# First row group's second edges loaded as float8 by pairs of units, and the packed exponentials' upper half written by ScalarE

## The chip, the cores and the metric

The kernel runs on one core of one Trainium2 chip. The metric is the device time of one execution in microseconds, the median of the runs. TensorE is called PE, VectorE DVE, ScalarE ACT, GpSimd POOL and the queue of SyncE SP. 16 DMA engines move the data of all queues.

## What is computed

A graph attention layer over 8192 nodes with 128 features, its input normalised and rectified first, and its output added to the input:

```python
    h = jnp.maximum(_layernorm(x, axis=-1), 0.0)
    Wh = h @ W
    a1, a2 = (a[:Fout, 0], a[Fout:, 0])
    f1 = Wh @ a1
    f2 = Wh @ a2
    e = jax.nn.leaky_relu(f1[:, None] + f2[None, :], negative_slope=ALPHA)
    e = jnp.where(adj == 0, -jnp.inf, e)
    attention = jax.nn.softmax(e, axis=1)
    h_prime = attention @ Wh
    x = x + h_prime
```

`x` is 8192 x 128 float32 (4.2 MB), `adj` is 8192 x 8192 int32 (268 MB) and holds only 0 and 1. ALPHA is 0.2.

## The kernel before

**Tiling.** The 8192 rows of the output are cut into 16 row groups `q` of 512 rows, four rows (`PACK`) to each of the 128 partitions. The 8192 columns of a group are cut into 16 units `b` of 512 columns. For one unit DVE writes four tiles of weights (L987: the larger of two packed exponentials, and the smaller of that and the mark of the edge), and PE multiplies them into the four accumulators `acc` (L476 and L480, 16 of each in a unit), which takes 16 x 4 x 4 products in a group.

**Edges.** POOL's queue loads `adj` and turns the int32 into one byte on the way. In `masks` the four rows of a partition lie side by side. The edges of two rows are put into one byte and summed as integers on POOL (`mix`, L274, for the first group; `mix4` and `join` for the later ones), PE transposes the sums (L458), and ACT spreads them into `marks` (`unpack`, L685). For this the bytes of the two rows of a pair must carry different values. In the first group all four rows arrive as uint8 (0 or 1), one unit at a time (`load_part`, L256, 128 x 4 x 512 bytes), and ACT multiplies the rows of the second half by 200 (`second`, L702) before POOL adds. In later groups `load_half` loads the second of each pair as float8 already, whose 1.0 is the byte 60.

**The first group does more than the others.** While it runs, PE also makes the features of all nodes (L440 and the transposes L422), DVE takes the statistics of `x` (`statistics`, L913) and finishes the inverses of the deviation (`inverses`, L928 to L937), ACT takes roots, rectifies, copies `wh` out of PSUM and takes exponentials, and POOL normalises (L283) and scales (`scaled`, L330). `x` comes in six loads on SP's queue (L200), of 1, 1, 2, 2, 4 and 6 tiles of 512 rows; the last three wait until the edges of units 0, 1 and 3 have landed. I call them x3, x4 and x5. `statistics(4)` needs x3, `statistics(6)` x4 and `statistics(10)` x5.

**The packed exponentials.** For tile `g` ACT writes eight exponentials per partition into `exps` (L675) and four more into `tmp` (L676), which signals `exps_ready`. DVE's `pack` makes the upper half of `packed` from `exps` with a multiplication (L965), waits for itself, and makes the lower half from both (L966). POOL's `scaled` waits for `exps_ready` too; ACT's `high_part` (L764) waits for `scaled`, and ACT's `root`, for which DVE's `inverses` waits, stands behind `high_part`.

**Order.** Every engine's program is written out by hand. DVE's in unit `b` of the first group is: weights of unit `b+1` (in two halves, with `inverses` between the halves where `b+1` is 2, 5 or 9), `low_part` (L974), `pack(b+2)`, statistics. PE starts the products of unit `b` only when `low_part(b)` is done (`pair_ready`).

## Time and profile before

| | us |
|---|---|
| median of 3 runs | 772.83 (772.83 to 774.30) |
| the profiled execution, device time | 773.42 |
| its span, first to last instruction | 771.5 |

| engine | busy us | share of the span |
|---|---|---|
| PE (matmul) | 751.3 | 97% |
| PE (weight load) | 687.7 | 89% |
| DVE | 726.5 | 94% |
| ACT | 579.2 | 75% |
| POOL | 442.9 | 57% |

The time outside the span is 773.42 - 771.5 = 1.9 us. The clock granted to PE was 0.999 of full speed over the span. Of the chain that ended last 91% is PE's, 4% DVE's, 2% ACT's. The share of a whole span says little here: the first row group (to about 93 us) and the other fifteen have different limits, so that the tables are to be read by stretches.

### The profile page before, as it was taken

To read this page: it belongs to the slowest core of one execution; us is meant where nothing else is said; L and a number is where in the kernel's file an instruction comes from. 1 tells how busy PE (TensorE), PEld (TensorE's weight loads), DVE (VectorE), ACT (ScalarE), POOL (GpSimd) and SP (SyncE) were. 2 spreads that over 40 slices of the span, in tenths; PEclk is the share of its full clock that TensorE was granted. 3 is DMA by queue.
4 is the path that set the end of the run, shared out by engine and by line. 5 is a ranking of instruction groups with operands and counts; after the bars stand their busy time and mean duration, and the time that the engine had idled before them with its cause. 6 is when DMAs were issued, how large, how long until landed. Compare 5 with 4: busy or idle time off the path is not lost.

```text
span 771.5 us, 23891 instructions
## 1 busy us (share of the span) xinstructions
PE 751.3 (97%) x8676; PEld 687.7 (89%) x8676; DVE 726.5 (94%) x1183; ACT 579.2 (75%) x1139; POOL 442.9 (57%) x501
## 2 busy tenths in 40 slices
PE   6899899999999999999999999999999999999997
PEld 5789789999999999999999999999999999999986
DVE  6998899999999999999999999999999999999996
ACT  5889887777778777777877777777777777777762
POOL 8787865646646664664666456465655646564510
PEclk9999999999999999999999999999999999999999
DMA  9999899999999999999999999999999999997100
GB/s 171 179 105 108 85 114 128 108 114 120 107 126 100 116 93 113 108 100 114 97 121 94 118 97 99 112 104 121 90 120 93 99 111 102 115 97 82 19 15 18
DMA packets 48246, 79.70 MB, mean 103 GB/s; under 512 B 2834, under 2 KB 11732, under 8 KB 48212
## 3 DMA queue, kind: packets, MB, share of 16 engines
q0 software_dynamic: 41088, 67.12, 90.5%
q1 hardware_dynamic: 6976, 12.09, 4.6%
q8 instruction: 17, 0.28, 0.1%
q14 instruction: 17, 0.14, 0.1%
q10 hardware_dynamic: 148, 0.07, 0.0%
HBM read 276.37 MB, written 4.23 MB: 364 GB/s over the span
## 4 chain that ended last, share of the span: by engine, by line
PE 91%; DVE 4%; ACT 2%; DMA 1%; POOL 1%; issue 1%; DVEq 0%; ACTq 0%; POOLq 0%
PE acc L476 56%; PE acc L480 29%; PE stage L467 4%; DVE wt_ring L987 2%; PE stage L440 1%; DMA masks<-in_adj_dram 1%; DVE pairs L974 1%; PE stage L422 0%; ACT marks L727 0%; DVE stats L913 0%; PE stage L458 0%; POOL tmp L330 0%; POOL masks L274 0%; DVE xm L1082 0%; ACT wh L649 0%
## 5 line engine op out<-in xcount | busy, mean ns | idle before, releaser
L476 PE MATMUL acc<-pairs,wt_ring 128*128 128x258 f16 x4096 | 717.5, 274 | 4.9 <-DVE pairs L974 3.5
L987 DVE SCALAR_TENSOR_TENSOR wt_ring<-stage,packed,marks 128x512 f32<-128x512 f32 x1024 | 688.4, 744 | 30.9 <-PE acc L480 21.5
L480 PE MATMUL acc<-pairs,wt_ring 128*128 128x129 f16 x4096 | 697.7, 220 | 0.0
L476 PEld LDWEIGHTS acc<-pairs,wt_ring 128*128 128x128 f16 x4096 | 398.8, 98 | 56.2 <-DVE pairs L974 5.1
L480 PEld LDWEIGHTS acc<-pairs,wt_ring 128*128 128x128 f16 x4096 | 400.3, 98 | 4.9
L727 ACT ACTIVATE marks<-codes 128x512 uint16<-128x512 uint8 x480 | 274.6, 620 | 12.5
L717 ACT ACTIVATE codes<-stage 128x512 uint16<-128x512 uint8 x240 | 142.8, 595 | 147.1 <-PE stage L467 146.6
L291 POOL DMA_DIRECT2D masks<-in_adj_dram x120 | 87.7, 731 | 219.8 <-PE stage L467 198.9
L310 POOL TENSOR_TENSOR masks<-masks 128x512 int32<-128x512 int32 x120 | 150.6, 1282 | 1.3
L319 POOL TENSOR_TENSOR masks<-masks 128x256 int32<-128x256 int32 x120 | 87.6, 735 | 55.7 <-ACT masks L710 54.8
L710 ACT ACTIVATE masks<-masks 128x512 uint16<-128x512 uint16 x120 | 74.8, 623 | 1.3 <-POOL masks L310 0.7
L467 PE MATMUL stage<-ident,masks 128*128 128x128 f32 x240 | 67.0, 279 | 0.8 <-ACT codes L717 0.4
L467 PEld LDWEIGHTS stage<-ident,masks 128*128 128x128 f32 x240 | 33.7, 141 | 5.0 <-issue 1.5
L337 POOL TENSOR_SCALAR fin<-fin 128x516 f32<-128x516 f32 x15 | 22.8, 1519 | 2.1 <-ACT fin L752 1.6
L330 POOL TENSOR_TENSOR tmp<-wh,tmp 128x512 f32<-128x512 f32 x16 | 18.0, 1124 | 10.0 <-ACT tmp L676 10.0
L440 PE MATMUL stage<-wx,ht 128*128 128x130 f32 x120 | 20.9, 299 | 1.5 <-ACT ht L643 0.7
L283 POOL TENSOR_SCALAR xn<-xm,small 128x128 f32<-128x128 f32 x42 | 19.4, 471 | 4.3 <-DVE small L937 4.3
L752 ACT ACTIVATE fin<-acc 128x258 f32<-128x258 f32 x60 | 19.4, 381 | 0.0
L347 POOL TENSOR_TENSOR xm<-fin,xm 128x512 f32<-128x512 f32 x15 | 18.0, 1199 | 1.8 <-ACT fin L758 1.5
L758 ACT ACTIVATE fin<-fin,inv 128x128 f32<-128x128 f32 x60 | 19.0, 392 | 0.0
L440 PEld LDWEIGHTS stage<-wx,ht 128*128 128x128 f32 x120 | 16.6, 200 | 2.7 <-ACT ht L643 1.1
L685 ACT ACTIVATE marks<-stage 128x1024 uint16<-128x1024 uint8 x16 | 16.3, 1019 | 1.4 <-PE stage L458 1.4
(78 smaller groups left out, 201.3 us busy)
## 6 DMA issues: line engine op xcount, KB each, us to landing
masks<-in_adj_dram POOLq DMA_DIRECT2D x120, 512.0 KB, 9.7
masks<-in_adj_dram POOLq DMA_DIRECT2D x16, 256.0 KB, 21.9
out_dram<-xm SPq DMA_DIRECT2D x15, 256.0 KB, 7.8
ht<-e_words SPq DMA_DIRECT2D x14, 256.0 KB, 8.5
xm<-in_x_dram SPq DMA_DIRECT2D x1, 1536.0 KB, 13.4
xm<-in_x_dram SPq DMA_DIRECT2D x2, 512.0 KB, 6.6
xm<-in_x_dram SPq DMA_DIRECT2D x1, 1024.0 KB, 9.8
xm<-in_x_dram SPq DMA_DIRECT2D x2, 256.0 KB, 3.1
```

The lines of the kernel that those rows point to most:

```text
L291: nc.gpsimd.dma_start(to[:, c * PACK + h:(c + 1) * PACK:2, :], adj_half[q, c, :, h::2, :]).then_inc(adj_second[c] if h else adj_loaded[c], 16)
L310: nc.gpsimd.tensor_tensor(edges4[:, c, :, 0, sl], edges4[:, c, :, 0, sl], edges4[:, c, :, 1, sl], ALU.add).then_inc(s["mixed4"], 1)
L319: nc.gpsimd.tensor_tensor(edges4[:, c, 0, 0, sl], edges4[:, c, 0, 0, sl], edges4[:, c, 1, 0, sl], ALU.add).then_inc(s["joined"], 1)
L337: nc.gpsimd.tensor_scalar(fin[:, :, E1:2 * E1], fin[:, :, E1:2 * E1], 1.0 / LOW, None, ALU.mult).then_inc(s["lows_scaled"], 1)
L440: mm = nc.tensor.matmul(to[:, r * 256:r * 256 + WC], ht[:, g % 2, k:k + P], wx[:], start=(r == 0), stop=(r == 1), skip_group_check=True)
L467: nc.tensor.transpose(stage[:, 0, 0:P], words[:, c * PACK, kk * P:(kk + 1) * P], ident[:]).then_inc(s["transposed"], 1)
L476: return nc.tensor.matmul(acc[:, r, 0:2 * E1], wtv[:, w, r, 1, :], pairv[:, t, :, 0:E1], start=st, stop=end)
L480: return nc.tensor.matmul(acc[:, r, E1:2 * E1], wtv[:, w, r, 0, :], pairv[:, t, 0, 0:E1], start=False, stop=False)
L710: nc.scalar.activation(twos[:, c, 1, 0, sl], twos[:, c, 1, 0, sl], ACT.Copy, scale=2.0).then_inc(s["doubled"], 1)
L717: nc.scalar.activation(codes2[:, b % 2, :].rearrange("p (s w) -> p s w", s=PACK), stage[:, 0, 0:P].bitcast(U8).rearrange("p (w s) -> p s w ...
L727: mm = nc.scalar.activation(split[:, b % MR, :].rearrange("p (s a w) -> p a s w", s=PACK, a=2)[:, h], codes[:, b % 2, :].rearrange("p (s w ...
L987: nc.vector.scalar_tensor_tensor(out=wtq[:, t % NW], in0=e_row, scalar=packed[:, t, 1:2], in1=edges[:, k], op0=ALU.max, op1=ALU.min).then_ ...
```

## The change

The rows of the second half are loaded as float8 (byte 60 for an edge), so that `second` goes; `SPLIT` becomes 256/60 for `unpack`. A load now covers one unit for units 0 and 1 and two units from there (`UNITS`), and is made of two DMAs, one for each half of the rows, that add to one semaphore (32). The counts before and behind POOL's other work (`EARLY`, `PARTS`) are in loads. ACT writes the upper half of `packed` with an exponential of its own (bias `log(SCALE * CUT)`), between the two that it had; DVE's multiplication goes.

```diff
-CUT = 1.0 - 2.0 ** -11
+CUT = 1.0 - 2.0 ** -11 - 2.0 ** -16
...
-SECOND = 200.0
-SPLIT = 256.0 / SECOND
+ONE8 = 60.0
+SPLIT = 256.0 / ONE8
...
-    EARLY = 10
+    EARLY = 5
...
-    PARTS = {0: (12,), 1: (13,), 2: (14, 15)}
+    PARTS = {0: (6,), 1: (7,), 2: (8,)}
+
+    UNITS = [(0, 1), (1, 2)] + [(u, u + 2) for u in range(2, UN, 2)]
...
-        adj_first = adj.rearrange("(q p s) (b k) -> q b p s k", p=P, s=PACK, k=BANK)
+        adj_first = adj.rearrange("(q p s) k -> q p s k", p=P, s=PACK)
...
-            for k, part in ((3, 0), (4, 1), (5, 3)):
-                sp.wait_ge(first_loaded[part], 16)
+            for k, part in ((3, 0), (4, 1), (5, 2)):
+                sp.wait_ge(first_loaded[part], 32)
                 load_x(k)
...
-            def load_part(u):
-                c, k = u // KC, u % KC
-                nc.gpsimd.dma_start(masks[:, c * PACK:(c + 1) * PACK, k * BANK:(k + 1) * BANK],
-                                    adj_first[0, u]).then_inc(first_loaded[u], 16)
+            def load_part(k):
+                lo, hi = UNITS[k]
+                c = lo // KC
+                at, to = (lo - c * KC) * BANK, (hi - c * KC) * BANK
+                for h, tiles in ((0, masks), (1, masks8)):
+                    sl = slice(HALF * h, HALF * (h + 1))
+                    nc.gpsimd.dma_start(tiles[:, c * PACK + HALF * h:c * PACK + HALF * (h + 1), at:to],
+                                        adj_first[0, :, sl, lo * BANK:hi * BANK]).then_inc(first_loaded[k], 16)
...
-                pool.wait_ge(first_loaded[u], 16)
-                pool.wait_ge(s["second_ready"], u + 1)
+                pool.wait_ge(first_loaded[part_of(u)], 32)
...
                 nc.scalar.activation(exps, wh[:, sl, Fo:WC], ACT.Exp, scale=1.0 - SLOPE, bias=cst[:, 0:1])
+                nc.scalar.activation(packedv[:, sl, :, 1], wh[:, sl, Fo:WC], ACT.Exp, scale=1.0 - SLOPE,
+                                     bias=cst[:, 3:4])
                 nc.scalar.activation(tmp[:, g % 2, :, Fo:E1], wh[:, sl, E1:WC], ACT.Exp, scale=-1.0,
                                      bias=cst[:, 1:2]).then_inc(s["exps_ready"], 1)
...
-            def second(b):
-
-                c, k = b // KC, b % KC
-                act.wait_ge(first_loaded[b], 16)
-                sl = slice(k * BANK // 2, (k + 1) * BANK // 2)
-                nc.scalar.activation(twos[:, c, 1, :, sl], twos[:, c, 1, :, sl], ACT.Copy, scale=SECOND
-                                     ).then_inc(s["second_ready"], 1)
...
-                then(nc.vector.tensor_scalar(packedv[:, sl, :, 1], exps, CUT / LOW, None, ALU.mult))
```

All calls of `second` go from ACT's program. POOL's program from its first load on, in the kernel before (a row is a line, its operation, its tiles, its shape and how many stand in a row):

```order
L256 DMA masks<-in_adj_dram 128x4x512 x2
L261 MEMSET ident 128x128
L263 ISA
L263 AFFINE_SELECT ident<-ident 128x128
L256 DMA masks<-in_adj_dram 128x4x512 x8
L274 TENSOR_TENSOR masks<-masks 128x2x128
L330 TENSOR_TENSOR tmp<-wh,tmp 128x4x128
L283 TENSOR_SCALAR xn<-xm,small 128x128 x6
L274 TENSOR_TENSOR masks<-masks 128x2x128
L330 TENSOR_TENSOR tmp<-wh,tmp 128x4x128
L256 DMA masks<-in_adj_dram 128x4x512 x2
L274 TENSOR_TENSOR masks<-masks 128x2x128
```

and in the changed one, where the loads are on L264, `mix` on L280, `scaled` on L336 and the normalisation on L289:

```order
L264 DMA masks<-in_adj_dram 128x2x512 x2
L268 MEMSET ident 128x128
L270 ISA
L270 AFFINE_SELECT ident<-ident 128x128
L264 DMA masks<-in_adj_dram 128x2x512 x2
L264 DMA masks<-in_adj_dram 128x2x1024 x6
L280 TENSOR_TENSOR masks<-masks 128x2x128
L336 TENSOR_TENSOR tmp<-wh,tmp 128x4x128
L289 TENSOR_SCALAR xn<-xm,small 128x128 x6
L280 TENSOR_TENSOR masks<-masks 128x2x128
L336 TENSOR_TENSOR tmp<-wh,tmp 128x4x128
L264 DMA masks<-in_adj_dram 128x2x1024 x2
```

The number of DMAs ahead of the first `mix` is ten in both, and now they cover eight units in place of ten. Behind the third and the fourth `scaled` one DMA stood in the kernel before; now two stand there.

ACT's program in the loop's first round (`b` = 0), in the kernel before, from `high_part(1)` to the normalisation of tile 4:

```order
L764 ACTIVATE pairs<-tmp 128x4x129
L649 ACTIVATE wh<-stage 128x260
L702 ACTIVATE masks<-masks 128x2x256
L776 ACTIVATE small<-stats,cst 128x8
L779 ACTIVATE small<-small 128x8
L643 ACTIVATE ht<-stage 128x512
L649 ACTIVATE wh<-stage 128x260
L675 ACTIVATE stage<-wh,cst 128x8
L676 ACTIVATE tmp<-wh,cst 128x4
L685 ACTIVATE marks<-stage 128x1024
L702 ACTIVATE masks<-masks 128x2x256
L635 ACTIVATE xn<-xm,small 128x128
```

and in the changed one:

```order
L762 ACTIVATE pairs<-tmp 128x4x129
L654 ACTIVATE wh<-stage 128x260
L774 ACTIVATE small<-stats,cst 128x8
L777 ACTIVATE small<-small 128x8
L648 ACTIVATE ht<-stage 128x512
L654 ACTIVATE wh<-stage 128x260
L680 ACTIVATE stage<-wh,cst 128x8
L681 ACTIVATE packed<-wh,cst 128x8
L683 ACTIVATE tmp<-wh,cst 128x4
L692 ACTIVATE marks<-stage 128x1024
L640 ACTIVATE xn<-xm,small 128x128
```

The two `second` (L702) are gone, and the new exponential (L681) stands ahead of the one that signals `exps_ready`, and ahead of the unpacking of the marks.

## Rows read from the trace of the kernel before

**Rows 1.** Windows: start:end, length; PE, PEld, DVE, ACT, POOL busy; PEclk; DMA; GB/s

```profile
15.00:30.00 15.00, 11.01 (x97) 8.81 (x95) 13.39 (x36) 12.42 (x32) 11.45 (x18) 1.00 1.16 206
30.00:45.00 15.00, 13.49 (x139) 12.33 (x140) 14.76 (x37) 12.59 (x30) 12.28 (x19) 1.00 1.21 137
...
97.00:760.00 663.00, 662.97 (x7822) 608.96 (x7823) 638.21 (x969) 499.81 (x956) 365.13 (x386) 1.00 0.95 101
```

**Rows 2.** Timeline of PE, 15 to 65 us: start, us, instruction, idle before it

```profile
30.47 0.28 PE L476 MATMUL acc<-pairs,wt_ring 128*128 128x258 f16 x1 [1.65 <-DVE pairs L974]
...
44.89 0.29 PE L476 MATMUL acc<-pairs,wt_ring 128*128 128x258 f16 x1 [0.86 <-DVE pairs L974]
...
63.01 0.28 PE L476 MATMUL acc<-pairs,wt_ring 128*128 128x258 f16 x1 [0.57 <-DVE pairs L974]
```

**Rows 3.** Timeline of DVE, 15 to 45 us, same columns

```profile
16.87 1.43 DVE L913 BATCH_NORM_STATS2 stats<-xm 128x6 f32<-128x256 f32 x4
19.03 2.73 DVE L987 SCALAR_TENSOR_TENSOR wt_ring<-stage,packed,marks 128x512 f32<-128x512 f32 x4 [0.73 <-ACT marks L685]
...
23.38 1.42 DVE L913 BATCH_NORM_STATS2 stats<-xm 128x6 f32<-128x256 f32 x4
24.71 1.39 DVE L987 SCALAR_TENSOR_TENSOR wt_ring<-stage,packed,marks 128x512 f32<-128x512 f32 x2
26.02 0.33 DVE L928 TENSOR_SCALAR small<-stats 128x8 f32<-128x8 f32 x1
...
28.10 1.40 DVE L987 SCALAR_TENSOR_TENSOR wt_ring<-stage,packed,marks 128x512 f32<-128x512 f32 x2
29.42 0.99 DVE L974 SCALAR_TENSOR_TENSOR pairs<-pairs,tmp 128x516 f16<-128x516 f16 x1
...
34.51 0.17 DVE L965 TENSOR_SCALAR packed<-stage 128x8 f16<-128x8 f32 x1
34.71 0.17 DVE L966 SCALAR_TENSOR_TENSOR packed<-packed,stage 128x8 f16<-128x8 f16 x1
34.79 1.44 DVE L913 BATCH_NORM_STATS2 stats<-xm 128x6 f32<-128x256 f32 x4
```

**Rows 4.** Timeline of ACT: `second` of unit 2; the exponentials behind 56.5 us

```profile
20.00 0.62 ACT L702 ACTIVATE masks<-masks 128x512 uint16<-128x512 uint16 x1
...
56.99 0.27 ACT L675 ACTIVATE stage<-wh,cst 128x8 f32<-128x8 f32 x1
57.20 0.29 ACT L676 ACTIVATE tmp<-wh,cst 128x4 f32<-128x4 f32 x1
```

**Rows 5.** Timeline of POOL, 20 to 30 us

```profile
20.77 0.72 POOL L274 TENSOR_TENSOR masks<-masks 128x256 int32<-128x256 int32 x1 [0.95 <-ACT masks L702]
...
28.81 1.05 POOL L330 TENSOR_TENSOR tmp<-wh,tmp 128x512 f32<-128x512 f32 x1 [0.39 <-ACT tmp L676]
```

**Rows 6.** Windows of three mixtures of transfers (last two columns: DMA share, GB/s)

```profile
13.50:21.00 7.50, 6.31 (x48) 5.32 (x47) 6.74 (x14) 6.30 (x18) 6.09 (x11) 1.00 1.13 241
...
36.00:40.00 4.00, 3.82 (x42) 3.37 (x41) 3.97 (x10) 3.75 (x9) 3.98 (x7) 1.00 1.24 105
127.00:133.00 6.00, 6.00 (x73) 5.51 (x72) 5.93 (x10) 4.02 (x8) 4.26 (x5) 1.00 1.06 163
```

**Rows 7.** Line L200, x3 with x4, then x5: issue, and time to landing

```profile
L200 SPq DMA_DIRECT2D xm<-in_x_dram x2: 380/383/386, 9.8 to 12.3; - x2
...
DMA to landing us min/median/max: 6.9/8.3/9.8
...
L200 SPq DMA_DIRECT2D xm<-in_x_dram x1: 381/381/381, 21.7 to 21.7; - x1
...
DMA to landing us min/median/max: 13.4/13.4/13.4
```

**Rows 8.** Line L256, the loads of units 2 and 3: duration of the issue, landing

```profile
L256 POOL DMA_DIRECT2D masks<-in_adj_dram x2: 742/758/774, 4.0 to 4.8; - x2
...
DMA to landing us min/median/max: 12.2/14.6/17.0
```

More of the change, by code:

```diff
@@ L50 @@
 SCALE = 0.015
-CUT = 1.0 - 2.0 ** -11
+CUT = 1.0 - 2.0 ** -11 - 2.0 ** -16
 TOP = 512.0
 NORM = 1.01
-SECOND = 200.0
-SPLIT = 256.0 / SECOND
+ONE8 = 60.0
+SPLIT = 256.0 / ONE8
 ABOVE = 0.1
-ONE8 = 60.0
 APART = 64.0
@@ L100, in batch_of, with part_of @@
         return next(k for k, (lo, hi) in enumerate(BATCHES) if lo <= g < hi)
+    def part_of(u):
+        return next(k for k, (lo, hi) in enumerate(UNITS) if lo <= u < hi)
     with ExitStack() as ctx:
@@ L128, in gat_kernel @@
         a_row = sb("a_row", [2, P], F32)
-        cst = sb("cst", [P, 3], F32)
+        cst = sb("cst", [P, 4], F32)
         stats = sb("stats", [P, NB, 3], F32)
@@ L149, in gat_kernel @@
             "adj_second0", "adj_second1", "adj_second2", "adj_second3",
-            *(f"first_loaded{u}" for u in range(UN)),
+            *(f"first_loaded{k}" for k in range(len(UNITS))),
             "ident_zero", "ident_ready", "cst_ready", "rows_done", "out_stored", "x_again",
@@ L155, in gat_kernel @@
             "scaled_ready", "high_ready", "pair_ready",
-            "second_ready", "mixed", "marked", "mixed4", "doubled", "joined", "taken", "lows_scaled", "sums_ready", "inv_ready", "fin_scaled", "limits_ready", "limits_turned", "flag_ready",
+            "mixed", "marked", "mixed4", "doubled", "joined", "taken", "lows_scaled", "sums_ready", "inv_ready", "fin_scaled", "limits_ready", "limits_turned", "flag_ready",
             "transposed", "weighted", "spent", "acc_done", "acc_free",
@@ L160, in gat_kernel @@
         adj_second = [s[f"adj_second{c}"] for c in range(NC)]
-        first_loaded = [s[f"first_loaded{k}"] for k in range(UN)]
+        first_loaded = [s[f"first_loaded{k}"] for k in range(len(UNITS))]
         x_loaded = [s[f"x_loaded{k}"] for k in range(len(LOADS))]
@@ L251, in load @@
                     adj_loaded[c] if r < 2 else adj_second[c], 16)
-            def load_part(u):
-                c, k = u // KC, u % KC
-                nc.gpsimd.dma_start(masks[:, c * PACK:(c + 1) * PACK, k * BANK:(k + 1) * BANK],
-                                    adj_first[0, u]).then_inc(first_loaded[u], 16)
+            def load_part(k):
[6 more added lines that the diff above has]
+                                        adj_first[0, :, sl, lo * BANK:hi * BANK]).then_inc(first_loaded[k], 16)
             load_part(0)
-            load_part(1)
             nc.gpsimd.memset(ident[:], 0.0).then_inc(s["ident_zero"], 1)
@@ L264, in _ @@
                                     pattern=[[-1, P]], channel_multiplier=1).then_inc(s["ident_ready"], 1)
-            for u in range(2, EARLY):
-                load_part(u)
+            for k in range(1, EARLY):
+                load_part(k)
             def mix(u):
                 c, k = u // KC, u % KC
-                pool.wait_ge(first_loaded[u], 16)
-                pool.wait_ge(s["second_ready"], u + 1)
+                pool.wait_ge(first_loaded[part_of(u)], 32)
                 sl = slice(k * P, (k + 1) * P)
@@ L355, in _ @@
             load_part(EARLY)
-            load_part(EARLY + 1)
             for b in range(UN):
@@ L370, in _ @@
                     scaled(b + 2)
-                for u in PARTS.get(b, ()):
-                    load_part(u)
+                for k in PARTS.get(b, ()):
+                    load_part(k)
                 if b in FIRSTS:
@@ L666, in exponentials @@
                 if g == 0:
-                    act.wait_ge(s["cst_ready"], 3)
+                    act.wait_ge(s["cst_ready"], 4)
                 if g == 0:
@@ L770, in root @@
                 if k == 0:
-                    act.wait_ge(s["cst_ready"], 3)
+                    act.wait_ge(s["cst_ready"], 4)
                 if k == 0:
@@ L793, in _ @@
             root(0)
-            second(0)
             exponentials(0)
@@ L803, in _ @@
             exponentials(1)
-            second(1)
             relu(2)
@@ L814, in _ @@
                     root(ROOTS[b])
-                if b + (2 if b == 0 else 3) < UN:
-                    second(b + (2 if b == 0 else 3))
-                elif b >= UN - 2:
+                if b >= UN - 2:
                     double(0, b - UN + 2, b - UN + 3)
@@ L827, in _ @@
                     unpack(b + 2, b + 2, first=True)
-                if b == 0:
-                    second(3)
                 if b + 4 < NQ:
@@ L1013, in _ @@
             nc.vector.memset(cst[:, 2:3], EPS).then_inc(s["cst_ready"], 1)
+            nc.vector.memset(cst[:, 3:4], float(math.log(SCALE * CUT))).then_inc(s["cst_ready"], 1)
             statistics(0)
```

## The prediction

> **What bounds the kernel now.** I read the windows by stage first [rows 1]. From 97 to 760 us PE is busy 662.97 of 663.00 us: the fifteen later groups are bound by PE, and the change leaves them as they are. What it can move is the first group. From 15 to 30 us PE is without work for 3.99 us, from 30 to 45 for 1.51, while DVE is busy 13.39 and 14.76 of 15. PE's timeline says what it waits for [rows 2]: for DVE's `low_part` (L974) 1.65 us before the products of unit 2 (30.47), 0.86 before unit 5 (44.89) and 0.57 before unit 9 (63.01). Behind unit 5 PE goes without a gap up to unit 9. So a microsecond that DVE saves or loses before 44.89 us moves the end, as long as nothing else takes its place. DVE's timeline [rows 3] shows what it does there: weights, `low_part`, `pack` and the statistics of `x`.
>
> **The change part by part.**
>
> `second` goes from ACT: 16 times 0.62 us [rows 4]. Most of it was covered, since ACT had idle time. Before 19 us it isn't: `second`, `mix`, transposes, marks and weights follow each other there, and DVE's weights of unit 1 (19.03) had waited 0.73 us for marks. Between nothing and the whole 0.62 us of an instruction can be won there; I take 0.4, since part of it lies beside PE's products, if the statistics between the weights are not late.
>
> `pack` loses one DVE instruction. From L965 to L966 it is 34.71 - 34.51 = 0.20 us [rows 3]. Six packs lie in the stretch from 16 to 45 us, 1.2 us in all, if nothing else is late.
>
> ACT gets one exponential more per tile. From L675 to L676 it is 57.20 - 56.99 = 0.21 us [rows 4], and it stands ahead of `exps_ready`. POOL's `scaled`, ACT's `high_part` and `root`, and DVE's `inverses` follow in a chain behind that signal. POOL's L330 at 28.81 us waited for L676 [rows 5]. Where that chain is what ends last (the inverses ahead of unit 5 and of unit 9) it costs up to 0.2 us each, and at the handover to the second group about 0.05, where POOL would wait for other work anyway. I take 0.2 before unit 9 and 0.05 there; bounds 0 and 0.4.
>
> POOL gets two more DMAs up to 31 us (18 for 16), 0.74 us each [rows 8]. POOL is busy 11.45 and 12.28 of 15 us there [rows 1] and waits for L676 [rows 5]: its idle time hides them, and I cost them at 0, with a bound of 0.4 for a `mix` that comes late.
>
> The loads are the part that decides. How the queues share the 16 engines can be read from three windows [rows 6]. With edges alone 105 GB/s are written, that is 420 GB/s read as int32. With x3 and x4 beside loads of single units (rows of 512 int32 = 2 KB, like `x`'s rows of 2 KB) 241 GB/s are written. With X for `x` and A for the edges as read, X + A/4 = 241 and X + A = about 410 give X = 185 and A = 225: about one to one. x3 and x4 have 1.57 MB and run from about 13.3 to 21.5 us, 191 GB/s, which agrees. From 127 to 133 us a store and a load of 256 KB each, with rows of 2 KB, run beside edge loads with rows of 8 KB: X + A/4 = 163 and X + A = 410 give X = 81, A = 329, one to four. So the queues take turns row by row, and whoever has longer rows gets more. The changed kernel reads the edges from unit 2 on in rows of 1024 int32 = 4 KB, beside the same `x` rows. One to two gives X = 410 / 3 = 137 and A = 273 GB/s. The Trainium skill ("DMA: Bandwidth & Descriptors", section "Queues, rings and completion order") says that an engine goes round the queues packet by packet; the trace agrees, since 1:1 turns into 1:4 with rows four times as long. The same page (section "Bandwidth") has larger transfers come out faster by themselves, to 78% of the peak at 1 MB; the trace doesn't bear it out where the queue is full (105 GB/s in units of 256 KB), and by it all loads here would be early and the sum would be a gain.
>
> *x3* (0.52 MB) landed at 9.8 + 6.9 = 16.7 us [rows 7]; it needs 3.8 us of data in place of 2.8, so 17.7. DVE's L913 at 16.87 waits until then and ends at 19.1. With that the weights of unit 1 start at 19.15 in place of 19.03: the gain of the start is gone.
>
> *x4* landed at 12.3 + 9.8 = 22.1. x3 and x4 take 1.57 / 0.137 = 11.5 us from 13.3, to 24.8, and with the tail of 0.6 us that it had, x4 is there at 25.4. DVE asked for it at 23.38 [rows 3]. Now its statistics run from 25.4 to 26.8, the first half of the weights of unit 2 to 28.1, and the inverses, which filled the 2.08 us from 26.02 to the second half at 28.10, waits included, take 0.8 to 1.2 us behind that: an estimate for five small instructions (L966, as small, took 0.17) without and with a stall beside POOL. The second half then starts at 28.9 to 29.3 in place of 28.1, and PE starts unit 2 at about 31.4 in place of 30.47: **0.9 us later**.
>
> *x5* was issued at 21.7 and landed 13.4 us later, at 35.1. DVE's second pair of statistics in the row at 34.79 started at about 35.5, 0.4 behind. Now the pair of units 2 and 3 lands before unit 3 did (21.8 us [rows 8]): 0.9 us at 420 GB/s and 1.7 MB at 273 end at 19.6. So x5 is issued 2 us earlier and follows x4 without a gap, 24.8 + 11.5 = 36.3, and with a tail of 0.6 to 1.6 us it lands at 36.9 to 37.9, I take 37.3. The statistics that need it start 1.85 us later than in the trace, and the weights of unit 4 and PE's unit 4 with them: **about 1.8 us later**, in which the 0.9 is contained.
>
> From there DVE gets back 0.2 us by `pack` and, of the 0.86 us that PE waited before unit 5, an estimated 0.15, because DVE's inverses now find their root ready. PE's unit 5 is then 1.45 us late (46.3). Behind it PE is the bound and gives nothing back. With 0.2 before unit 9 and 0.05 at the handover the sum is 1.8 - 0.35 + 0.25 = 1.7 us. The profiled execution took 773.42 us (span 771.5 and 1.9 around it), and would take 775.1; the median of the runs shown is 772.83, 0.6 below it, and I forecast **774.5 us**, 0.22% above before. A tail of 0.6 or 1.6 us for x5, inverses that stall beside POOL's second DMA, and exponentials at 0 or 0.4 give this case 0.9 to 2.6 us, 773.7 to 775.4.
>
> The pairs cost unit 2 nothing by this sum: `mix(2)` started at 20.77 [rows 5] and its pair lands at 19.6.
>
> **The rivals.**
>
> *Nothing that can be measured.* The queues share by bytes and the 1:4 came from elsewhere. Then x3, x4 and x5 come when they came, but the pair of units 2 and 3 lands only at 21.8, and `mix(2)` is 1.0 us later than 20.77 and runs beside DVE's inverses, of which each may have to wait for the other: DVE's L974 at 29.42 took 0.99 us beside POOL's L330, which had begun at 28.81 [rows 3, 5]. The Trainium skill ("SBUF — State Buffer", section "SBUF: two separate sides") calls the port that both share an exclusive lock for a whole instruction; the trace agrees: L330 ended at 29.86 and L974 only at 30.41. The gain of the start (0.4) and of two or three packs (0.5) goes into that and into the exponential's 0.2 at three places: -0.3 to +1.0, I take +0.3, 773.1 us. For it: the share was read from two mixtures and this is a third. Against it: both fit one rule.
>
> *Faster.* x isn't what DVE waits for, and the pair is early. Then the start gives 0.4, the packs 0.6 to 0.8 before unit 5, where PE has 0.86 us to give, and the added exponential takes 0.2: 1.0 us less, 771.8, at most 1.9 less. This asks for x5 by 34.5 us, against 35.1 before, with more in its way; it decides from that point. Only the earlier issue of x5 speaks for it.
>
> *The change doesn't do what it says*: float8 rows could be dearer than uint8 ones. The later groups load one of each, and the windows with them write at the same 101 to 105 GB/s [rows 1, 6]; I give it no chance of its own.
>
> **How the numbers follow.** About 0.2% (1.5 us) is what a measurement of this kernel can tell from no change. The forecast's case has a chance of 0.60 and lies on both sides of that bound: 0.37 above it and 0.23 below. The second case has 0.27, nearly all of it within the bound, the third 0.13, of which 0.07 are faster by more than 0.2%. Faster 0.07, same 0.54, slower 0.39. The range takes in the second case whole and the upper part of the third one out: 772.2 to 775.8.
>
> **What would show it.** In the changed kernel's trace x4's landing at about 25.4 and x5's at about 37.3 (its issue at 19.6); 205 GB/s in place of 241 beside `x`; DVE idle for about 2 us before the statistics of tiles 6 and 10, with a DMA as what ended it; PE's idle time before units 2 and 4 longer, and PE's unit 5 at 46.3. Wrong would be: 241 GB/s as before, x5 at 35 or earlier, and DVE without a wait for a DMA behind 16 us. The exponential is right if the distance from ACT's first to its third in a tile is 0.41 in place of 0.21 us.

## The result, and the profile after

The changed kernel takes **777.72 us** (776.84 to 778.38), the kernel before 772.88 us beside it: 4.8 us slower. The ratio, formed from all executions and not from the two medians, is **1.0056, 95% interval [1.0044, 1.0068]**. The forecast was 774.5 us and its range ended at 775.8, so the sign of the sum was right and the size was not.

The profiled execution took 778.38 us against 773.42, 4.96 more. These lie in two places:

| | before | after | difference |
|---|---|---|---|
| profiled execution, us | 773.42 | 778.38 | +4.96 |
| its span, us | 771.5 | 774.8 | +3.3 |
| time outside the span, us | 1.9 | 3.6 | +1.7 |

The four executions after have 3.4 to 3.6 us outside the span, the kernel before had 1.8 to 2.2 in every execution for which the span is known, so the +1.7 is sure. The span itself scatters more: 773.4 to 774.8 us after (median 774.2), and before about 771.0 to 771.7 in the median.

The profiled executions also start unlike. x3, which waits for the edges of unit 0, was issued at 9.8 us before and at 9.1 after, and at 9.0 to 10.8 in the five kernels (after is one) whose loads are the same up to there. A difference of under 1 us between two single profiles at one place therefore says little; a distance within one profile is steadier.

Windows of after, with the columns of [rows 1]:

```profile
15.00:30.00 15.00, 10.33 (x94) 8.30 (x94) 11.01 (x32) 10.20 (x27) 11.49 (x19) 1.00 1.09 202
30.00:45.00 15.00, 13.22 (x120) 12.06 (x121) 12.53 (x27) 9.41 (x25) 11.13 (x17) 0.89 1.11 147
```

DVE is busy 11.01 and 12.53 us of 15 where it was 13.39 and 14.76, and PE's granted clock is 0.89 from 30 to 45 us, where it was 1.00. The waits of PE before units 2, 5 and 9 answer to [rows 2]:

```profile
31.71 0.40 PE L481 MATMUL acc<-pairs,wt_ring 128*128 128x258 f16 x1 [2.97 <-DVE pairs L965]
31.91 0.31 PE L485 MATMUL acc<-pairs,wt_ring 128*128 128x129 f16 x1
...
32.99 1.18 PE L445 MATMUL stage<-wx,ht 128*128 128x130 f32 x4
33.96 1.06 PE L427 MATMUL stage<-ident,xn 128*128 128x128 f32 x4
...
35.65 0.66 PE L445 MATMUL stage<-wx,ht 128*128 128x130 f32 x4
...
47.81 0.29 PE L481 MATMUL acc<-pairs,wt_ring 128*128 128x258 f16 x1 [0.98 <-DVE pairs L965]
...
65.99 0.28 PE L481 MATMUL acc<-pairs,wt_ring 128*128 128x258 f16 x1 [0.64 <-DVE pairs L965]
```

Unit 2 starts 1.24 us late (31.71 for 30.47), unit 5 2.92 late, unit 9 2.98. Between unit 2 and unit 5 another 1.7 us are lost, and the first lines show what happened there: behind 2.97 us without work a product (L481) takes 0.40 to 0.42 us in place of 0.27, the features (L445) 1.18 in place of 0.66. The windows have the clock:

```profile
31.00:32.00 1.00, 0.28 (x2) 0.22 (x3) 1.00 (x4) 0.00 (x0) 0.98 (x2) 0.86 1.08 201
32.00:35.00 3.00, 3.00 (x17) 2.71 (x16) 3.00 (x7) 0.39 (x1) 1.74 (x4) 0.50 1.10 208
35.00:36.00 1.00, 1.00 (x12) 0.93 (x10) 0.64 (x2) 0.60 (x1) 0.00 (x0) 0.93 1.06 187
```

PE ran from 32 to 35 us at a granted clock of 0.50, the lower of its two levels (1.2 in place of 2.4 GHz), and began 17 instructions in these 3 us where it began 36 before. From the first product of unit 2 to the second features it took 35.65 - 31.71 = 3.94 us, and before 2.29.

DVE's timeline of after, beside [rows 3]:

```profile
17.47 1.43 DVE L905 BATCH_NORM_STATS2 stats<-xm 128x6 f32<-128x256 f32 x4 [1.16 <-DMA xm<-in_x_dram]
...
25.64 1.42 DVE L905 BATCH_NORM_STATS2 stats<-xm 128x6 f32<-128x256 f32 x4 [2.62 <-DMA xm<-in_x_dram]
...
30.46 1.20 DVE L965 SCALAR_TENSOR_TENSOR pairs<-pairs,tmp 128x516 f16<-128x516 f16 x1
...
37.49 0.17 DVE L957 SCALAR_TENSOR_TENSOR packed<-packed,stage 128x8 f16<-128x8 f16 x1 [1.85 <-ACT tmp L683]
37.57 1.42 DVE L905 BATCH_NORM_STATS2 stats<-xm 128x6 f32<-128x256 f32 x4
```

The first two statistics wait for x, as forecast. The third pair (37.57) has no wait for a DMA ahead of it: there `pack` waited 1.85 us for ACT's exponential (L683), which waited for PE's slow features. x's loads themselves (issue, then time to landing), beside [rows 7]:

```profile
L204 SPq DMA_DIRECT2D xm<-in_x_dram x1: 386/386/386, 9.1 to 9.1; - x1
DMA to landing us min/median/max: 8.4/8.4/8.4
...
L204 SPq DMA_DIRECT2D xm<-in_x_dram x1: 380/380/380, 12.1 to 12.1; - x1
DMA to landing us min/median/max: 13.5/13.5/13.5
...
L204 SPq DMA_DIRECT2D xm<-in_x_dram x1: 380/380/380, 19.2 to 19.2; - x1
DMA to landing us min/median/max: 18.6/18.6/18.6
```

The last of it lies behind the last recorded instruction. A window from 1 us ahead of the span's end to 7 us behind it, in 40 slices of 0.2 us, has only packets of an instruction queue, 8 KB each:

```profile
GB/s 0 0 0 0 0 0 0 41 0 0 0 0 0 0 0 0 0 0 0 41 0 0 0 0 0 0 0 0 0 0 0 0 0 0 0 0 0 0 0 0
DMA packets 2, 0.02 MB, mean 2 GB/s; under 512 B 0, under 2 KB 0, under 8 KB 0
## 3 DMA queue, kind: packets, MB, share of 16 engines
q14 instruction: 2, 0.02, 0.6%
```

They move 0.4 and 2.8 us behind the span's end. In the kernel before there are two as well, but at 0.2 and 1.4 us. So instructions are still loaded after the last recorded work, and now later.

### The profile page after: what moved, and what is told of

It reads as the page before. It is cut to its first block, busy times and chain, and to the rows that moved or that the text cites. A ratio compares the mean times of both kernels' runs of the same rounds, so it can differ in the third digit from the quotient of the medians.

```text
span 774.8 us, 23862 instructions
## 1 busy us (share of the span) xinstructions
PE 751.7 (97%) x8676; PEld 687.2 (89%) x8676; DVE 724.0 (93%) x1168; ACT 573.7 (74%) x1139; POOL 444.2 (57%) x503
## 4 chain that ended last, share of the span: by engine, by line
PE 91%; POOL 5%; issue 2%; ACT 2%; DVE 1%; DVEq 0%; POOLq 0%; ACTq 0%
PE acc L481 56%; PE acc L485 29%; PE stage L472 4%; POOL masks L264 2%; PE stage L445 1%; POOL xn L289 1%; POOL tmp L336 1%; POOL masks L280 1%; PE stage L427 0%; ACT marks L725 0%; ACT marks L692 0%; PE stage L463 0%; ACT wh L654 0%; DVE xm L1074 0%; POOL masks L316 0%
## 5 line engine op out<-in xcount | busy, mean ns | idle before, releaser
L481 PE MATMUL acc<-pairs,wt_ring 128*128 128x258 f16 x4096 | 718.0, 274 | 7.1 <-DVE pairs L965 5.6
L481 PEld LDWEIGHTS acc<-pairs,wt_ring 128*128 128x128 f16 x4096 | 399.0, 98 | 58.6 <-DVE pairs L965 7.5
L336 POOL TENSOR_TENSOR tmp<-wh,tmp 128x512 f32<-128x512 f32 x16 | 17.8, 1111 | 12.6 <-ACT tmp L683 12.5
L289 POOL TENSOR_SCALAR xn<-xm,small 128x128 f32<-128x128 f32 x42 | 19.9, 483 | 5.5 <-DVE small L929 5.5
L445 PE MATMUL stage<-wx,ht 128*128 128x130 f32 x120 | 21.0, 300 | 1.4 <-ACT ht L648 0.7
L445 PEld LDWEIGHTS stage<-wx,ht 128*128 128x128 f32 x120 | 16.6, 200 | 2.7 <-ACT ht L648 1.1
L905 DVE BATCH_NORM_STATS2 stats<-xm 128x6 f32<-128x256 f32 x32 | 11.8, 420 | 6.6 <-DMA xm<-in_x_dram 6.6
## 6 DMA issues: line engine op xcount, KB each, us to landing
xm<-in_x_dram SPq DMA_DIRECT2D x1, 1024.0 KB, 13.5
```

The source lines that it names most:

```text
L289: ins = nc.gpsimd.tensor_scalar(xn[:, g % 2, r * P:(r + 1) * P], xm[:, g, r * P:(r + 1) * P], small[:, 5, t:t + 1], small[:, 6, t:t + 1], ...
L445: mm = nc.tensor.matmul(to[:, r * 256:r * 256 + WC], ht[:, g % 2, k:k + P], wx[:], start=(r == 0), stop=(r == 1), skip_group_check=True)
L481: return nc.tensor.matmul(acc[:, r, 0:2 * E1], wtv[:, w, r, 1, :], pairv[:, t, :, 0:E1], start=st, stop=end)
```

## The experiments: what each part costs

Sixteen kernels were timed beside the kernel before (773.0 to 773.8 us). The theory after the result: late x loads cost the span, the fall of PE's clock adds about as much again, and the added exponential brings the time outside. Rivals: the exponential or `mix` delays the first group, or the number of DMAs does.

**The pairs alone** (`b_pairs`): the kernel before with its first group's edges loaded by pairs of units from unit 2 on, all as uint8 in one DMA, multiplication kept.

```
-                nc.gpsimd.dma_start(masks[:, c * PACK:(c + 1) * PACK, k * BANK:(k + 1) * BANK],
-                                    adj_first[0, u]).then_inc(first_loaded[u], 16)
+                nc.gpsimd.dma_start(masks[:, c * PACK:(c + 1) * PACK, at:to],
+                                    adj_first[0, :, :, lo * BANK:hi * BANK]).then_inc(first_loaded[k], 16)
```

> The kernel before with one part of the change alone: the edges of units 2 to 15 are loaded by pairs (rows of 1024 int32 = 4 KB in place of 2 KB), as uint8 and with the multiplication on ACT kept, one DMA for each pair. Theory of the rows (queues take turns row by row, so that longer rows of edges slow x): beside x about 205 GB/s are written in place of 241, x4 lands near 25.5 us and x5 near 37.5 us, PE waits about 3 us before unit 2, its clock falls to half behind that, and the span is 2.5 to 4 us longer than before. Rival (the loss comes from the split into two DMAs, from float8 or from the added exponential): x4 at 22 us, x5 at 35 us and a span within 0.7 us of before.

Measured: 777.09 us, ratio 1.0048 [1.0036, 1.0061], 1.9 to 2.0 us outside the span. x4 was issued at 11.7 and took 13.8 us, x5 at 18.8 and 19.1. The pairs alone bring 3.3 us, without float8, without the exponential and without more DMAs. In the profiled execution, the fastest of the five (775.76), PE's clock was kept (PE idle 2.54 us before unit 2), and x5 is what is late last, as the prediction had it. PE's unit 5 starts at 47.01 there, 2.1 us later than before, with the clock at 1.00 throughout.

**More DMAs, rows as before** (`b_two`, one execution): each unit in two DMAs of half the rows, rows of 2 KB.

> The kernel before with each unit's load split into two DMAs of half the rows (uint8 both, rows of 2 KB as before, multiplication kept), 32 DMAs in place of 16, POOL issuing 22 more of its time's 0.74 us until 41 us. Theory of the rows: x4 lands within 0.7 us of 22.1 us, since the rows' length is unchanged, and 240 GB/s are written beside x. Rival (it is the split that slows x): about 205 GB/s. Theory L in its form that the number of DMAs brings the time outside the span: device time less span above 3 us.

Measured: 780.74 us with 1.6 outside the span. It is slow for a reason of its own: POOL issues up to 16 more DMAs and is busy all of the 15 us from 30 to 45, and PE waits for its `mix` (L277) 6.9 us in all. What it tells is in x's loads:

```profile
L200 SPq DMA_DIRECT2D xm<-in_x_dram x1: 386/386/386, 10.4 to 10.4; - x1
DMA to landing us min/median/max: 6.9/6.9/6.9
...
L200 SPq DMA_DIRECT2D xm<-in_x_dram x1: 381/381/381, 12.9 to 12.9; - x1
DMA to landing us min/median/max: 9.8/9.8/9.8
...
L200 SPq DMA_DIRECT2D xm<-in_x_dram x1: 380/380/380, 22.2 to 22.2; - x1
DMA to landing us min/median/max: 13.2/13.2/13.2
```

6.9, 9.8 and 13.2 us, against 6.9, 9.8 and 13.4 before [rows 7]. The number of DMAs leaves x alone; the length of the rows decides. (The size of one DMA doesn't: `after` loads 256 KB at a time from unit 2 on, as the kernel before does, and x4 takes 13.5 us beside it.)

**A late x4 alone** (`b_xlate`): before, with one number changed.

```
-            for k, part in ((3, 0), (4, 1), (5, 3)):
+            for k, part in ((3, 0), (4, 2), (5, 3)):
```

> The kernel before with the load x4 alone issued later: it waits for the edges of unit 2 (16.2 us) in place of unit 1 (12.3 us). Nothing else differs. Theory (a late x4 is the cost by itself): x4 lands near 25.8 us, x5 at 35 us as before, PE is idle for about 3 us before unit 2, the granted clock is at half for some microseconds behind it, and PE's unit 5 starts 2.5 to 3 us later than before's 44.89; the span grows by about 3 us. Rival (x4 is hidden, and what costs is x5, or the exponential): PE's unit 5 within 0.7 us of before.

Measured: 776.48 us (774.23 to 776.9), ratio 1.0033 [1.0021, 1.0045]. In the profiled execution PE idled 2.95 us before unit 2 (30.99) and then ran at a granted clock of 0.50 up to 36.9 us, the mark of after in a kernel that has none of the change's parts. The lateness of x is enough for both. x5 was in time here (34.2 us), so x's second wait doesn't hide the fall: from unit 2 to unit 5 PE took 16.99 us, before 14.42. The executions agree: one with a mean clock of 0.999 has a span of 772.1, the five with 0.995 to 0.997 have 773.8 to 774.8.

**The exponential alone** (`b_exp`): before, with ACT's third exponential and without DVE's multiplication.

```
+                nc.scalar.activation(packedv[:, sl, :, 1], wh[:, sl, Fo:WC], ACT.Exp, scale=1.0 - SLOPE,
+                                     bias=cst[:, 3:4])
...
-                then(nc.vector.tensor_scalar(packedv[:, sl, :, 1], exps, CUT / LOW, None, ALU.mult))
```

> The kernel before with the other part of the change alone: ACT writes the upper half of the packed exponentials, DVE's multiplication goes. Two things are open. In the span: the forecast has ACT's exponential at up to 0.2 us before units 5 and 9 and DVE's pack at 0.2 us less per tile, so the span is 771.3 to 772.0 (before: 771.5). Outside the span the device time of before holds 1.9 us, that of the three kernels with the whole change 3.3 to 3.6. Theory E (the exponential brings this): device time less span is 3.3 us or more here. Theory L (the split float8 loads bring it): 1.9 us here.

Measured: 775.32 us, ratio 1.0026 [1.0016, 1.0037], of it 3.4 to 3.7 us outside the span in each of 8 executions: the split float8 loads, this expectation's theory L, aren't needed for that. The span is 771.3 to 772.5, in the median 0.25 above before's. 1.9 us for this part and 3.3 for the pairs are 5.2, against 4.8 for both together.

## The experiments: x and the clock

**PE kept busy** (`a_fill`): after, with 44 products more, ahead of PE's wait for unit 2, into columns that nobody reads.

```
+                if b == 2:
+                    for _ in range(44):
+                        nc.tensor.matmul(acc[:, 3, 2 * E1:2 * E1 + P], pairv[:, 0, 0, 0:P], pairv[:, 0, 0, 0:P],
+                                         start=False, stop=False, skip_group_check=True)
```

> The changed kernel with 44 more products on PE ahead of its wait for unit 2, into columns of PSUM that nothing reads (about 2.5 us of PE work in the stretch in which it was idle for 2.97 us). They change no result. Theory (the idle stretch let PE's clock fall to half, and the slow products and features of unit 2 behind it cost 1.6 us): the granted clock stays at 1.00 from 30 to 36 us, the exponentials of tile 4 on ACT come 1.5 us earlier, the statistics of tiles 9 and 10 then wait for x5 (37.8 us), so that of the 1.6 us at most 0.5 reach PE's unit 5: span 0.3 to 0.8 us shorter than the changed kernel's 774.8. Rival (the clock's fall costs its full 1.6 us at the end): span 773.2. Second rival (no effect of the clock): span unchanged.

Measured: 778.2 us, ratio 1.006 [1.0047, 1.0073], no gain; the spans are 774.7 to 774.9, also in the one of the five executions whose mean clock was 1.000. From 29 us on the clock was 1.00, but it had fallen to 0.50 from 26 to 28 us, ahead of the filled stretch. The added products then ended at about 32.8 us, 1.1 behind the end of DVE's `low_part`, so that they held unit 2 up themselves, and the third statistics now waited 0.72 us for x5 (38.44). This didn't isolate the clock, but it shows what stands behind it: x5.

**x issued earlier** (`a_xearly`): after, with x3 at 7.0 us, x4 with unit 0 and x5 with unit 1.

```
-            for k, part in ((3, 0), (4, 1), (5, 2)):
+            sp.wait_ge(s["mean_ready"], 2)
+            load_x(3)
+            for k, part in ((4, 0), (5, 1)):
```

> The changed kernel, but with the three last loads of x issued earlier: x3 when DVE has read x's second tile (about 7 us) in place of unit 0's landing, x4 with unit 0's landing, x5 with unit 1's. The bytes and the rows are the changed kernel's. Theory (x's lateness is the whole loss): the data of x3 begin near 10.4 in place of 13.3 us, x4 lands near 22 and x5 near 34 us, DVE no longer waits for a DMA before the statistics of tiles 6 and 10, PE's clock stays, PE's unit 5 starts at 44.3 to 45.3 us (before: 44.89), and the span is 771 to 772.5. Rival (exponential and POOL's added DMAs cost as much): the span stays above 773.

Measured: 775.51 us, ratio 1.0032 [1.002, 1.0045]. The profiled span is 771.8 us, 3.0 less than after and 0.3 above before; clock 1.00, PE's wait before unit 2 1.69 us, before unit 5 0.98 (at 44.70, where before had 44.89). Outside the span it still has 3.2 to 3.6 us. By medians the span is 772.1, against 774.2 after and 771.7 for before in the same round. So nearly all of the span's loss is x's lateness and what follows from it.

**The same on before** (`b_xearly`).

> The kernel before with the three last loads of x issued earlier, as in the changed kernel with earlier loads. In the kernel before DVE waited for x nowhere behind 16 us, so the theory that x matters only when it is late has nothing gained: span 771.2 to 771.8. Rival (x was late in the kernel before too, at tile 10): span 770.8 or less.

Measured: 774.15 us, ratio 1.0015 [1.0006, 1.0024]. No gain: ACT's `second` waits 5.3 us in all for the edges that x displaced. The earlier issue repairs a fault of after and isn't a gain by itself.

**The same with the multiplication back** (`a_xearly_noexp`): a_xearly without the added exponential.

> The changed kernel with the earlier loads of x and with the upper half of the packed exponentials made by DVE again: the loads are the only part of the change left. Theory E: device time less span falls from 3.4 back to 1.9 us. Theory L: it stays at 3.4 us. In the span: the exponential costs nothing or gains a little where DVE is the limit, so 771.5 to 772.3, against 771.8 with it.

Measured: 774.39 us, ratio 1.0013 [1.0003, 1.0023], 1.7 to 2.0 us outside the span. The span is 1.2 us above a_xearly's in the profiled execution, in which POOL's `mix` waited 4.3 us for edges (1.4 in a_xearly) and PE's clock was at 0.50 from 25 to 28 us; the medians of the spans are 772.5 and 772.1, so that the two kernels can't be told apart there. This is the best kernel with the new loads, and it doesn't beat before.

**x one step earlier, no exponential** (`a_x0_noexp`): x3 and x4 with unit 0, x5 with unit 1.

> The kernel after with VectorE's multiplication back, no exponential added, and x's loads issued one step earlier than in after: the fourth and fifth when unit 0 is in, the sixth when unit 1 is in. The fourth load's own issue stays at 9.1 us, so that units 1 and 2 are less delayed than where it was issued at 7 us (there GpSimd waited 4.3 us in all for the second edges). Theory (x's landing and unit (2,3)'s are both in time): span 771 to 772, 1.6 to 2.1 outside it, 773.2, level with before. Rival (whichever bytes go first, the others are late, since the queues are full until 40 us): 774.4 as with the loads at 7 us.

Measured: 776.99 us, ratio 1.0049 [1.0037, 1.0061]; both theories missed. PE idled 3.24 us before unit 2 in the profiled execution and ran at about 0.50 from 32 to 35 us. x4, issued at 9.8 us in place of 12.1, took 15.6 us and landed at 25.4, as in after: it comes behind x3 (17.6 us), and 1.05 MB in 7.8 us are 134 GB/s, near the 137 that the prediction gave to x. To issue the later load earlier moved nothing, while a_xearly, which issued x3 at 7.0, had x4 at 23.6. The six executions split: one of 774.5 us with a span of 772.6 and a mean granted clock of 0.999, five of 776.8 to 778.0 with spans of 774.9 to 776.4 and 0.996 to 0.997. The same program, 2.3 us or more apart, and the mean clock apart with it.

## The experiments: the time outside the span

Three theories, with letters of their own: L, the added exponential brings it; K, the fourth constant and its wait; M, the instructions that DVE's program lost.

**The constant alone** (`b_cst4`): before with `cst` of four columns, a fourth memset and ACT's waits on 4.

> The kernel before with the fourth constant alone: `cst` four columns wide, a fourth memset, ScalarE's two waits on 4 in place of 3; VectorE's multiplication is kept and ScalarE has no further exponential. The question is what brings the 1.6 us outside the span that every kernel with the added exponential has (measured time less span 3.3 to 3.6 us, against 1.6 to 2.1 without it). Theory K (the constant and its wait do it): 774.6, 3.3 to 3.6 outside the span. Theory L (the added exponential, or what its missing partner on VectorE leaves, does it): 773.1, 1.6 to 2.1 outside.

Measured: 772.82 us, ratio 0.9997 [0.9989, 1.0006], 1.8 to 2.2 outside. K falls.

**Exponential and multiplication both** (`b_both`): b_exp with this line back.

```
+                then(nc.vector.tensor_scalar(packedv[:, sl, :, 1], exps, CUT / LOW, None, ALU.mult))
```

> The kernel before with ScalarE's exponential into the upper half added and VectorE's multiplication kept as well: it writes the same upper half over again behind ScalarE, so nothing is taken from VectorE. Theory M (the instructions that VectorE's program lost, 15 of 790, do it): 1.6 to 2.1 outside the span. Theory L (ScalarE's added exponential does it): 3.3 to 3.6 outside; either way the span itself 771.5 to 772.5, since both engines wait more than 0.4 us a tile on PE.

Measured: 773.7 us, ratio 1.001 [1.0001, 1.0019], 1.9 to 2.1 outside. L falls: ACT's exponential is there, the time outside is not.

**Exponential with the first constant** (`b_exp_c0`): b_exp without the fourth.

> The kernel before with ScalarE's exponential in place of VectorE's multiplication, but with the bias of the first constant, so that there is no fourth constant (the upper half is then written without the small factor under one that keeps its rounding down). Theory K (constant): 1.6 to 2.1 outside the span, time 773 to 774. Theory L (exponential or lost VectorE instructions): 3.3 to 3.6 outside the span, time 775.3. With the two runs above this tells apart constant, exponential and missing multiplication.

Measured: 774.93 us, ratio 1.0026 [1.0015, 1.0038], 3.3 to 3.5 outside. What is missing is DVE's 16 instructions. The windows at the end, b_both's first and then b_exp's, again 1 us ahead of the span's end in slices of 0.2 us:

```profile
GB/s 0 0 0 0 0 0 41 0 0 0 0 0 41 0 0 0 0 0 0 0 0 0 0 0 0 0 0 0 0 0 0 0 0 0 0 0 0 0 0 0
...
q14 instruction: 2, 0.02, 0.9%
```

```profile
GB/s 0 0 0 0 0 0 41 0 0 0 0 0 0 41 0 0 0 0 0 41 0 0 0 0 0 0 0 0 0 0 0 0 0 0 0 0 0 0 0 0
...
q14 instruction: 3, 0.02, 1.1%
```

b_exp loads one more block of instructions, 1.2 us behind the one before it. DVE's program ends in a branch that jumps over a long general path, so a theory F was formed: where the branch or its target lies among the blocks decides. (M' in the expectations is the rival that the multiplication itself matters.) Four kernels test it; the memsets write columns that nobody reads.

```
+            for k in range(15):
+                nc.vector.memset(cst[:, 4 + k:5 + k], 0.0)
```

`a_pad15` has them behind the four memsets at DVE's start:

> The kernel after with 15 memsets of a 128 x 1 column that nobody reads, put behind the four at VectorE's start, where it waits for x until 3.8 us anyway (0.03 us each). VectorE's program then has as many instructions ahead of the branch at its end as that of the kernel before has (16 multiplications went, one memset came). Theory F (where the branch at the program's end and its target lie among the blocks in which instructions are loaded decides it): 1.6 to 2.1 us outside the span, time 776.6. Theory M' (the multiplication itself, as an instruction between two waits, matters): 3.3 to 3.6 outside the span as in after, 778.2.

`a_pad8` has 8 there:

> The kernel after with 8 such memsets in place of 15, so 7 instructions fewer than before's program. Theory F says that the step lies at one count between 0 and 15 more: either 3.3 to 3.6 or 1.6 to 2.1 outside the span, nothing between them (778.2 or 776.6). A cost that goes with the number of instructions would give the middle, 2.6 and 777.4. Theory M': 3.3 to 3.6.

`a_padelse` has 15 in the path that the branch skips, never executed:

> The kernel after with 15 memsets inside the branch of VectorE's program that is not taken (the general path behind the flag), so never executed: they move the branch's target by 15 places and leave the branch itself where it is in after. Theory F with the target's place deciding: 1.6 to 2.1 outside the span, 776.6. Theory F with the branch's own place deciding, or theory M': 3.3 to 3.6, 778.2.

`a_xearly_pad` is a_xearly with 15 at the start:

> The kernel after with both repairs: x's loads issued earlier (the fourth at 7 us, the fifth with unit 0, the sixth with unit 1, which alone gave 775.5 with 3.4 outside the span) and the 15 memsets at VectorE's start. Theory F: span 771.8 to 773 as without them, 1.6 to 2.1 outside, 773.9, within 0.2% of before. Theory M': 775.5.

Measured: 776.5, 776.74, 776.49 and 775.2 us, ratios 1.0039 [1.0024, 1.0055], 1.0047 [1.0032, 1.0063], 1.0052 [1.0037, 1.0068] and 1.0027 [1.0015, 1.0039]. All 18 executions of these four have 1.7 to 2.0 us outside the span. Instructions that do nothing, even ones that never run, take 1.6 to 1.7 us away there (medians of 1.8 to 1.9 in place of 3.4 to 3.5), so it is the program's length and nothing it computes; 8 do as much as 15, so the effect isn't in proportion. The branch's own place isn't it, since a_padelse leaves that as in after. The four also widen `cst`; b_cst4, which does so by one column, shows no effect of it, more columns without instructions weren't tried. The first three gain only 1.0 to 1.2 us over after as a whole, as their spans, 774.7 to 775.0 in the median, are 0.5 to 0.8 longer than after's 774.2, within their scatter of 773.2 to 776.4. The window at the end of a_padelse:

```profile
GB/s 0 0 0 0 0 0 41 0 0 0 0 0 0 0 0 0 0 0 0 0 0 0 0 0 0 0 0 0 0 0 0 0 0 0 0 0 0 0 0 0
...
q14 instruction: 1, 0.01, 0.4%
```

In all 18 kernels of this case the last instruction packet tells the two kinds apart: 0.2 to 1.4 us behind the span's end in the thirteen with 1.6 to 2.2 us outside, 2.6 to 2.8 behind it in the five with 3.2 to 3.7 (after, a_fill, a_xearly, b_exp, b_exp_c0). The Trainium skill ("Runtime: NRT & Kernel Launch", section "Instruction fetch mechanics") says that a taken branch whose target isn't in the pages at hand forces a load of that page before the engine goes on; the traces agree with one load more or later, but that the branch is what forces it was argued, not tried, and where the boundary lies is open. a_xearly_pad missed its 773.9: the time outside went, but its span was 772.1 to 774.1, over a_xearly's 771.7 to 773.3. Why is open; its profiled execution had a granted clock of 0.89 from 15 to 30 us, and POOL's `mix` waited 4.0 us for edges in it.

The profiles of these kernels also do what a_fill could not. The work of a_padelse, a_pad8 and a_pad15 in the first group is that of after, and in a_padelse's profiled execution PE's clock held:

```profile
31.07 0.28 PE L481 MATMUL acc<-pairs,wt_ring 128*128 128x258 f16 x1 [2.65 <-DVE pairs L965]
...
41.40 0.29 PE L481 MATMUL acc<-pairs,wt_ring 128*128 128x258 f16 x1 [1.48 <-DVE pairs L965]
...
46.48 0.29 PE L481 MATMUL acc<-pairs,wt_ring 128*128 128x258 f16 x1 [0.56 <-DVE pairs L965]
...
64.64 0.28 PE L481 MATMUL acc<-pairs,wt_ring 128*128 128x258 f16 x1 [0.63 <-DVE pairs L965]
```

```profile
37.17 0.77 DVE L905 BATCH_NORM_STATS2 stats<-xm 128x6 f32<-128x256 f32 x2 [1.14 <-DMA xm<-in_x_dram]
```

Now the third statistics do wait for x5, PE waits before unit 4, and unit 5 starts at 46.48. In a_pad8 PE had waited just as long before unit 2, and its clock fell:

```profile
31.98 0.29 PE L481 MATMUL acc<-pairs,wt_ring 128*128 128x258 f16 x1 [2.65 <-DVE pairs L965]
...
48.08 0.29 PE L481 MATMUL acc<-pairs,wt_ring 128*128 128x258 f16 x1 [0.98 <-DVE pairs L965]
```

```profile
33.00:36.00 3.00, 3.00 (x18) 2.67 (x17) 2.91 (x5) 0.98 (x2) 1.09 (x3) 0.50 1.10 206
```

So did a_pad15's, behind 2.22 us (unit 2 at 32.81, unit 5 at 48.90). From unit 2 to unit 5 the three with the fall took 16.10 (after), 16.10 and 16.09 us, and the two with the full clock in that stretch 15.41 (a_padelse) and 15.40 (a_fill). **With x5 as late as it was, the clock's fall costs 0.7 us at unit 5**, not its full 1.65: the rest lies beside the wait for x5.

a_padelse's span is 773.2 and its execution 775.04 us. It goes by the path that the prediction worked out; that it also meets its 46.3 for unit 5 and its 775.1 us is in part luck, since in this execution x4 and x5 landed at 24.9 and 37.2 us, 0.7 and 0.6 earlier than in after. The kernel's other three executions had mean clocks of 0.994 to 0.997 and spans of 773.9 to 776.4.

## Why the prediction was wrong, point by point

**What bounds the kernel: right.** From 97 to 760 us PE is busy 662.55 of 663 us after, 662.97 before; all that changed lies in the first group and outside the span.

**The loads: right, within 0.5 us.** The turn by rows, worked out from two mixtures, held for the third. 205 GB/s were forecast for the rows of 4 KB, and from 20 to 35 us 204 were written. x3 was forecast for 17.7 and landed at 17.5, x4 25.4 and 25.6, x5 37.3 and 37.8. b_pairs has the lateness without the rest, and b_two shows that rows and not DMAs make it. The second case (sharing by bytes) and the third (x5 by 34.5) fall with this.

**Unit 2, 0.9 us late: 1.24.** x4's statistics ran from 25.64 us (forecast 25.4), the inverses took 0.85 (0.8 to 1.2), and the second half of the weights started at 29.14 (28.9 to 29.3), 1.04 later than before. The other 0.2 is DVE's `low_part`, which took 1.20 us (0.99 before). POOL's `scaled` had ended by then (30.25), but two DMA issues of POOL stood beside it (30.20 to 31.70), the second of them added by the change; no run changes that alone. The first late statistics (17.47 for 16.87) cost nothing behind them: the weights of unit 1 started at 18.8, before at 19.0.

**Unit 5 at 46.3: 47.81. This step failed.** The sum priced PE's longer wait as a delay and nothing else. It had forecast the idle time itself: 1.65 us before, and 0.9 more; it was 2.97. But behind the 2.97 us PE's clock fell to half, and the 3 us of work behind it took 1.65 us longer. That held up the exponentials of the next tile, so `pack` came late (37.49), and x5's lateness lay beside it: the two don't add. 1.24 and 1.68 are the 2.92 at unit 5.

How much of the missing 1.5 us is the clock's follows from the distance between unit 2 and unit 5. The forecast has 46.3 - 31.4 = 14.9 us. With the full clock it was 15.4, with the fall 16.1. So 0.3 came up to unit 2 (31.71 for 31.4); 0.5 lie on the path over x5, which landed 6.1 us behind unit 2's start where the forecast had 5.9, and on which the 0.35 us that DVE and PE were to give back didn't show; and 0.7 are the clock's. b_pairs, at full clock, has unit 5 at 47.01 and bears out that the delay alone was put too low.

No row of before could show the fall, since behind its start PE's longest wait was 1.65 us with the clock at 1.00. But the clock's column was among the rows, and the price of half a clock behind a longer wait should have been a bound of the range: 1.65 us for the 3 us that it lasted here, up to 2.6 where it lasted 6 with x5 in time (b_xlate).

**The time outside the span: carried over as 1.9, was 3.6. The second step that failed.** The prediction added what lies around the span as a constant. It depends on the code: DVE's 15 or 16 instructions fewer bring 1.3 to 1.7 us, shown by b_exp and b_exp_c0 against b_both, and by the padded kernels against after.

**The smaller terms.** The exponential's distance from first to third was forecast at 0.41 us and is 0.40:

```profile
28.44 0.27 ACT L680 ACTIVATE stage<-wh,cst 128x8 f32<-128x8 f32 x1
28.64 0.29 ACT L681 ACTIVATE packed<-wh,cst 128x8 f16<-128x8 f32 x1
28.84 0.29 ACT L683 ACTIVATE tmp<-wh,cst 128x4 f32<-128x4 f32 x1
```

In the span it cost 0.25 to 0.55 us by medians (b_exp, b_exp_c0, and b_both, where DVE's work isn't even taken away); the forecast had 0.25. What `pack` and `second` save was hidden, as DVE waits for x. PE's wait before unit 9 grew by 0.07, not 0.2. Whether the further DMAs on POOL cost the 0.2 us of `low_part` above is open.

So the sum closes: 775.1 forecast for the profiled execution, 1.5 for unit 5 (0.7 of it the clock's) and 1.7 outside give 778.3; it was 778.38.

## What to carry to other kernels

Transfers that run side by side shared the engines by the length of their rows: before lengthening one, work out when the other now lands, and issue it earlier, its first load above all (a_xearly against a_x0_noexp). Where a change makes PE's longest wait longer, read the granted clock behind waits and put half the clock for the next microseconds into the range; a lateness that comes later may hide part of it. A kernel's time isn't its span: compare the two in every execution. Where the difference between them moved, look at the instruction queues behind the last work, and try a few idle instructions before you blame what the edit computes.

## What the runs showed of the hardware

- **Rows set the share.** Beside x's rows of 2 KB, edge rows of 2 KB let x4 land in 9.7 to 10.7 us (six kernels that issue it with unit 1), rows of 4 KB in 13.3 to 13.8 (six), whether the edges came in one DMA (b_pairs) or two (after).
- **PE's clock falls behind a wait, not at a fixed length of it.** Behind 2.65 us it held in a_padelse and fell in a_pad8, with the same work in the first group. It held behind 2.54 (b_pairs), and fell behind 2.22 (a_pad15), 2.50 (b_two, where the products are slow from 50.4 to 53.8 us), 2.95 (b_xlate), 2.97 (after) and 3.24 (a_x0_noexp), and in a_fill at 25 us behind waits of 1.35 and 0.58. Executions of one program differ in it too, to judge by their mean clocks, and can lie over 2 us apart.
- **What the fall costs depends on what stands behind it.** From unit 2 to unit 5 it cost 0.7 us where x5 was late too (16.1 for 15.4), and where x5 was in time PE took 2.6 us more than before (b_xlate, 16.99 for 14.42, half the clock for 6 us).
- **Code has a tail.** Sixteen instructions fewer on DVE made the kernel 1.3 us longer behind its last work (b_exp_c0 against b_both: medians of 3.35 and 2.05 us outside the span); 15 instructions that are never executed took 1.6 back (a_padelse against after).
